# A chunk's product with its channel means moved from GpSimd to VectorE, and the steps of the last part put in a new order

## What is computed

```
s       = sum over the 8 channels of a group of z        # z: normalised x
idx     = argmax over positions of s
q_val   = z at idx
sim_max = sum over the 8 channels of q_val * z
gap     = mean over positions of z                       # one number per image and channel
sim_gap = sum over the 8 channels of gap * z             # "gapped" is the product gap * z
sim     = sim_max * D * zero + sim_gap * one             # D: Gaussian of the distance to idx
gate    = sigmoid((sim - mean) / std * weight + bias)    # std over the 49 positions
x3      = x + z * gate
x       = x3 + attention(groupnorm(x3))
```

## Time and profile before

| | before |
|---|---|
| median of 3 runs | 2124.77 us (2120.78 to 2130.49) |
| profiled execution, its time | 2115.13 us |
| its span | 2113.3 us |
| mean granted TensorE clock | 0.949 of full |
| TensorE busy | 1821.7 us, 86% |
| VectorE busy | 1367.5 us, 65% |
| ScalarE busy | 891.6 us, 42% |
| GpSimd busy | 166.5 us, 8% |

### The profile page before, as it was taken

How to read it: one execution, slowest core, us unless ns; L and a number is a source line. 1 busy time by engine, 2 the same in 40 slices (tenths; PEclk the granted TensorE clock), 3 DMA queues, 4 the chain that set the end, 5 groups by cost and what they waited for, 6 DMA issues and landing times. The chain is left out here.

```text
span 2113.3 us, 41985 instructions
## 1 busy us (share of the span) xinstructions
PE 1821.7 (86%) x16164; PEld 1230.7 (58%) x16164; DVE 1367.5 (65%) x2786; ACT 891.6 (42%) x2341; POOL 166.5 (8%) x61
## 2 busy tenths in 40 slices
PE   2699999999999999996877889999983589999998
PEld 1355555556666666664656667666661356666666
DVE  4667776675555555441333446787775899999994
ACT  0344444544444444452333434555441144443343
POOL 1000000000000000000000000000001233333331
PEclk9899999999999999998988999999995599999999
DMA  3112222264666666487878995664533001111101
GB/s 99 39 62 89 104 77 77 90 157 146 203 179 181 204 179 190 143 206 191 216 210 209 222 239 140 152 154 128 133 93 126 16 31 62 62 62 62 47 31 46
DMA packets 262635, 267.16 MB, mean 126 GB/s; under 512 B 208868, under 2 KB 234852, under 8 KB 262440
## 3 DMA queue, kind: packets, MB, share of 16 engines
q1 hardware_dynamic: 262280, 264.22, 44.2%
q0 software_dynamic: 160, 0.26, 0.0%
HBM read 148.84 MB, written 115.61 MB: 125 GB/s over the span
## 5 line engine op out<-in xcount | busy, mean ns | idle before, releaser
L499 DVE TENSOR_TENSOR vk<-p_vk,mask_vo 128x512 f32<-128x512 f32 x256 | 176.3, 688 | 464.1 <-PE p_vk L390 464.1
L426 PE MATMUL p_dw<-tw,qd 98*64 98x98 f32 x3072 | 244.3, 296 | 84.2 <-ACT agg_out L694 60.9
L426 PEld LDWEIGHTS p_dw<-tw,qd 98*64 98x64 f32 x3072 | 200.6, 206 | 148.1 <-ACT agg_out L694 79.7
L694 ACT ACTIVATE agg_out<-p_dw 128x294 f32<-128x294 f32 x256 | 106.4, 416 | 326.5 <-PE p_dw L426 250.8
L667 ACT ACTIVATE half_b<-p_qkv 98x384 f32<-98x384 f32 x256 | 125.2, 489 | 233.7 <-PE p_qkv L349 231.8
L452 PE MATMUL p_g<-o,w_proj 128*128 128x392 f32 x512 | 208.8, 533 | 3.0 <-DVE var L555 2.4
L349 PE MATMUL p_qkv<-w_qkv,half_a 128*98 128x384 f32 x512 | 190.4, 495 | 6.7 <-DVE half_a L571 6.7
L349 PE MATMUL p_qkv<-w_qkv,z_odd 128*98 128x384 f32 x512 | 191.6, 497 | 1.8 <-DVE z_odd L571 1.8
L402 PE MATMUL p_out<-vk,qr 128*49 128x136 f32 x2048 | 173.6, 291 | 8.3 <-DVE oN L514 5.2
L1485 POOL TENSOR_TENSOR gapped<-z,gate_gap 128x1568 f32<-128x1568 f32 x16 | 53.8, 3363 | 1599.0 <-DMA z<-z_scratch 1597.3
L702 ACT ACTIVATE o<-p_turn 128x196 f32<-128x196 f32 x256 | 85.2, 333 | 173.8 <-PE p_turn L411 172.9
(11 more groups left out here) (191 smaller groups left out, 3114.0 us busy)
## 6 DMA issues: line engine op xcount, KB each, us to landing
qkv_scratch<-half_b SPq DMA_DIRECT2D x32, 1176.0 KB
qd<-qkv_scratch SPq DMA_DIRECT2D x64, 588.0 KB
agg_scratch<-agg_out SPq DMA_DIRECT2D x128, 294.0 KB, 5.5
tw<-in_w_toep SPq DMA_DIRECT2D x128, 220.5 KB
half_a<-agg_scratch SPq DMA_DIRECT2D x48, 392.0 KB, 6.7
half_b<-agg_scratch SPq DMA_DIRECT2D x48, 392.0 KB, 6.6
half_a<-in_x SPq DMA_DIRECT2D x16, 784.0 KB, 4.7
x_scratch<-xb SPq DMA_DIRECT2D x16, 784.0 KB, 5.6
```

The source lines that it names most:

```text
L426: mm = pe.matmul(p_dw[NP * cp:NP * cp + NP, PR * s:PR * s + PR], qd[:, QB % 2, :, ch - QB_CH * qb], tw[:, SB % 2, :, 6 * (F % SB_FILLS) + ...
L499: v.tensor_tensor(dst[:, :, 0:128].rearrange("p k (c n) -> p k c n", c=HC), src[:, :, 0:2 * D].unsqueeze(2).to_broadcast([128, 4, HC, 2 * D]),
L694: a.activation(agg_out[:, DB % 2, at:at + 3, :].rearrange("p s n -> p (s n)"), p_dw[:, 0:3 * PR], ACT.Copy).then_inc(dw_ev, 1)
```

## The change

`gapped` is made by VectorE (`v_gapped`, chunk of age 1, between `v_ssq` and `v_context`) and no longer by GpSimd. GpSimd keeps its two `pow` steps. The lists of VectorE, TensorE and ScalarE are put in another order, and some steps move over the border between two rounds, with another age. No other instruction is added or taken away, no shape is changed, and nothing outside the last part is touched.

```diff
+        def v_gapped(v, it):
+            z2_there(v, it)
+            wait(v, "gap_mm", it)
+            done(v.tensor_tensor(by_image(gapped[:, :, :]), by_image(z2[it % Z2S][:, :, :]),
+                                 over_positions(W["gate_gap"][:, it, :, :]), ALU.mult), "gapped")
@@ v_round
-            run(v_dsum, 3)
+            run(v_hot, 2)
             run(v_scale, 5, 0)
             run(v_sim, 3)
+            run(v_sum, 4)
             run(v_x4, 6, 1)
+            run(v_picked, 2, 0)
+            run(v_centre, 4)
             run(v_ssq, 3)
-            run(v_centre, 4)
-            run(v_picked, 2, 0)
+            run(v_gapped, 1)
             run(v_context, 3)
             run(v_square_sum, 4)
             run(v_find, 1)
             run(v_max, 5)
             run(v_var, 4)
+            run(v_picked, 2, 1)
             run(v_gate, 3)
-            run(v_picked, 2, 1)
-            run(v_dist, 1)
+            run(v_dsum, 2)
             run(v_qv, 2)
             run(v_probs, 5)
             run(v_gated, 3, 0)
             run(v_prod, 2)
+            run(v_dist, 1)
             run(v_scale, 4, 1)
             run(v_gated, 3, 1)
-            run(v_hot, 1)
             run(v_x3, 3)
-            run(v_sum, 3)
             run(v_x4, 5, 0)
@@ pe_round
-            run(pe_gap, 2)
+            run(pe_gate, 4, 0)
             run(pe_turn, 6)
             run(pe_gate, 4, 1)
+            run(pe_out, 6, 0)
             run(pe_sim, 3)
-            run(pe_out, 6, 0)
             run(pe_out, 6, 1)
+            run(pe_fg, 5)
             run(pe_hot, 2, 0)
-            run(pe_fg, 5)
+            run(pe_sums, 1)
             run(pe_mean, 4)
             run(pe_hh, 5, 0)
-            run(pe_sums, 1)
             run(pe_scores, 5)
+            run(pe_hot, 2, 1)
             run(pe_hh, 5, 1)
-            run(pe_hot, 2, 1)
             run(pe_var, 4)
+            run(pe_gap, 1)
             run(pe_hh, 5, 2)
             run(pe_hh, 5, 3)
-            run(pe_gate, 3, 0)
@@ a_round
+            run(a_hh, 5, 1)
             run(a_gauss, 2)
-            run(a_sums, 1)
             run(a_tanh, 3)
-            run(a_hh, 5, 0)
-            run(a_hh, 5, 1)
             run(a_exp, 5)
             run(a_hh, 5, 2)
             run(a_hh, 5, 3)
             run(a_beta, 5)
-            run(a_sim_square, 2)
             run(a_gap, 1)
             run(a_fg, 4)
+            run(a_sim_square, 2)
+            run(a_sums, 0)
             run(a_square, 3)
+            run(a_hh, 4, 0)
@@ g_round (g_gapped is gone)
-            run(g_root, 6)
-            run(g_deviation, 4)
-            run(g_gapped, 2)
+            run(g_root, 5)
+            run(g_deviation, 3)
```

## The result

The changed kernel takes 2147.64 us (median of four runs, 2131.07 to 2153.94); the kernel before, on the same occasion, 2122.89 us (four runs, 2120.78 to 2130.49). The ratio is 1.011 with a 95% interval of 1.0055 to 1.0164. So it is slower by 1.1 to 1.2%, some 23 to 25 us. I had forecast +9 us and a range up to 2142. One execution of the kernel before, beside order_mended, fell in a slow state (2592.16 us, mean granted clock 0.645) and is left out of the ratios.

A forecast was written before the change was run, and what follows sets the result against it. VectorE was taken to bound the kernel. Full rounds +10.6 us, fill -2.0 and drain +0.5 sum to +9.1, so 2124 us by the profiled execution, 2134 us by the median; range 2116 to 2142 us.

The forecast's parts named there:

- VectorE bounds the kernel, and stands still for GpSimd in `sstd_eps`: Full rounds: VectorE sets the 27.20 us round and stalls 1.75 us for `gapped`; the product on VectorE adds 1.70 us.
- The root is held by the product ahead of it: GpSimd's root of `ssq` waits for `v_gapped`; VectorE idles 1.01 us per round, rounds of 28.16 us; chance 0.74.
- The extrapolation from 0.05 us in the earlier trace and 0.73 us in the earlier trace: Small delays of the other root and of `gapped` on GpSimd taken as one hold, giving 1.49 us for the root.
- The rule of the Trainium skill: VectorE instruction with two SBUF inputs and GpSimd instruction reading SBUF exclude each other; second blocks in full: round 1.01 us longer.
- Fill -2.0, drain +0.5: Outside the 11 full rounds: pipeline fill 2.0 us shorter, drain 0.5 us longer.
- The moves cost nothing as long as VectorE sets the round: New order of the engine lists priced at nothing; narrowest place `v_gated(3, 0)`, with 0.4 us to spare.
- TensorE falls to half clock: Rival: the wait ahead of `pe_var` grows to 2.4 us and the clock falls; +26 us in all, 2151 us; chance 0.04.
- The range: Median of 2116 to 2142 us: hold bounds, half of the case without a hold, and 3 us of scatter.

The follow-up runs named there:

- order_mended: Changed kernel with GpSimd's root started ahead of `zc`, ScalarE's squares ahead of its copies, and first `pe_gate` ahead of the last `pe_hh`: 2111.19 us, ratio 0.9977.
- product_only: Kernel before with its order kept; only `gapped` moved to VectorE, between `pick` and `context`: 2113.88 us, ratio 0.9977.
- gate_early: Changed kernel with the first `pe_gate` moved ahead of the last `pe_hh` in TensorE's list: 2125.93 us, ratio to the kernel before 1.0034.
- root_first: Changed kernel with `ssq` moved ahead of `mean`, `zc` and `pick` in VectorE's list: 2123.11 us, ratio to the kernel before 1.0006.
- the other occasion: Changed kernel run again unaltered beside the kernel before: 2142.42 us against 2119.1, ratio 1.0117.
- before_more: Kernel before with one more VectorE reduction (1.78 us, result unused) ahead of `square_sum`: 2145.25 us, ratio 1.0137.
- order_only: Changed kernel's order, but `gapped` left on GpSimd right behind its root of `ssq`: 2163.52 us, ratio 1.02.
- filler: Changed kernel with 8 more matmuls of unused result for TensorE ahead of `pe_var`: 2127.0 us, ratio to the kernel before 1.0048.

## Why the prediction was wrong

- *VectorE bounds the kernel, and stands still for GpSimd in `sstd_eps`*: right. The stall went with the product (0.17 us for 1.90), and product_only shows what it is worth without the new order: rounds of 27.16 us against a forecast of 27.15.
- *The root is held by the product ahead of it*: right in mechanism and size. 2.48 us for 2.50, 0.98 us lost for 1.01, rounds of 28.14 for 28.16. The extrapolation from 0.05 us in the earlier trace rows and 0.73 us in the earlier trace rows to 1.5 us carried. The rule of the Trainium skill (SBUF — State Buffer, Who interferes with whom) agrees with the trace where VectorE's product begins first, here also for an instruction on 4 numbers per partition. Where the root begins first the two differ: `zc` begins 0.05 us into a root of 1.01 us and takes its usual 1.79 us, and so it does in root_first and order_mended. There the measurement decides, and it is why it helps to let the root start first.
- *Fill -2.0, drain +0.5*: by the marks -3.1 in the fill; in the drain +3.1, of which 2.6 are a half-clock round. Near enough; without the clock the last part is 7.6 us longer by the profiles and 6.8 us by gate_early, for a forecast of 9.1.
- *The moves cost nothing as long as VectorE sets the round*: right for a TensorE at full clock, where no wait opened that I had not laid out. I had found `gated` with 0.4 us to spare (0.6 by the trace) and called that enough.
- *TensorE falls to half clock*: this is the step that failed. I named the wait (2.4 us ahead of `pe_var`), and it came as said. But I gave it 0.04, since 2.4 us is short, and I set the point from which it decides at 6.9 us of half clock per round, by the slack of the whole round, 3.46 us. What decides is the slack of the first deadline behind the wait: with 0.6 us to spare there, 1.2 us at half clock are enough, by my estimate. Spells of 6.8 us cost 2.6 us a round (30.72 - 28.14) and spells of 3.4 us 1.1 us (29.24 - 28.14), 13.6 us in all in the profiled execution, where my sum had nothing.
- *The range*: 2142 as its upper end took in the bounds of the hold and no part of the half clock. With the 13.6 us added, 2134 becomes 2148, close to the median of 2147.64; that it is so close is in part luck, since the rest was 7.6 us and not 9.1, and the other occasion gave 2142.42. The scatter of the changed kernel, 2131 to 2154 us, was wider than the 3 us that I had allowed for a median; its source is not shown.

## What to carry to other kernels

When an operation moves from GpSimd to VectorE, look at what GpSimd still does beside it: here a product of two SBUF tiles on VectorE held a root of 4 numbers on GpSimd almost to its end (2.48 us for 1.01), so put it where the reader of that root is far, or let the root start first. When a change makes TensorE wait longer in one piece, ask not how much slack its round has but how much the first consumer behind the wait has, and move that consumer's matmuls up; here one line moved was worth some 14 us by the traces. A step list that is tight at full clock is not yet a safe one. And where runs of one kernel scatter, compare the part that was changed by itself before giving the scatter a cause: here two profiled executions 5.3 us apart were alike in that part to 0.7 us.

## What was not expected of the hardware

TensorE's clock fell behind waits of 2.3 to 2.4 us in two different orders, and behind waits of 2.0 us in gate_early and 1.8 us in root_first, but not in every such round: the same wait was followed by full clock in one round and by 6.8 us at 1.2 GHz in another. Within one execution it settled into a pattern, four rounds in succession of 30.7 us with a spell in each. Why some rounds are spared was not settled by these runs. Nor do they part the one long wait from the idle time of TensorE in the round as a whole, which grows with it: without a spell 2.5 us in the kernel before, 3.7 in the changed one, 4.2 in before_more, 4.8 in order_only. The filler shortens both. With waits of 1.4 us and less it did not fall in the steady rounds of any of the profiled executions.
